# Results read back inside the merged scan and expert stage, and one PSUM bank for the up products with two for the down products

## The chip, the cores and the metric

The kernel runs on one core of a Trainium2 chip. The metric is the device time of one execution in microseconds; lower is better. Five engines run side by side, each working through its own queue in order: TensorE (PE; its weight loads are listed apart as PEld), VectorE (DVE), ScalarE (ACT), GpSimd (POOL), and SyncE (SP), which here only issues transfers. Work on one engine waits for work on another through semaphores. An engine whose next instruction waits does nothing else meanwhile.

## The reference

Eight layers over 4096 tokens of 128 numbers, each `x = layernorm(x + f(x))`. The change touches the last three:

```python
x = _layernorm(x + _L2_ffn_ref(x, ...))   # mixture of 8 experts, the best 2 of them per token
x = _layernorm(x + _L3_attn_ref(x, ...))  # selective state-space scan, see below
x = _layernorm(x + _L3_ffn_ref(x, ...))   # 8 dense experts, gated by top-p (0.8) probabilities

# _L3_attn_ref, shortened
x = resid * rsqrt(mean(resid**2) + EPS) * norm_w
skip = x @ skip_w.T;  xs = silu(causal_conv4(x @ in_w.T) + conv_b)
delta = softplus(xs @ wd1.T @ wd2.T + wd2_b)
h_l = exp(delta_l * A) * h_(l-1) + (delta_l * x_l) * B_l      # 16 states for each of 256 channels
y = (einsum(h, C) + xs * W_D) * silu(skip);  return resid + y @ out_w.T

# _L3_ffn_ref, shortened
h = relu(einsum('bth,ehf->betf', x, W1) + b1);  y = einsum('betf,efh->beth', h, W2) + b2
return einsum('bte,beth->bth', gate, y)
```

## The kernel before

The 4096 tokens are eight chunks of 512 (`NCH = 8`). `XT` holds the activations with the features on the partitions. PSUM has eight banks, `PS[0]` to `PS[7]`, each of 512 numbers per partition.

**Stage 6** is the expert mixture with two experts per token. It sorts tokens by expert into 72 tiles, and scatters each tile's result to DRAM (`result_d`) with indirect transfers from POOL. After the last tile comes a tail over the eight chunks: SP reads the two results of each token back (two transfers of 256 KB a chunk, into three buffers `YB`), DVE sums the two, PE turns the sum with four transposes, and DVE adds it to `XT` (`join`). A fence of all engines ends the stage.

**Stage 7** (`scan_moe_stage`) merges the last two layers. Everything in it is one list, `plan`, of steps; each engine walks the list and does its own part of each step, so the list fixes the order on every engine. After a prologue for chunks 0 and 1 it counts steps q from -8 to 319, and 32 steps make the scan of one chunk: for each of 16 states and 2 halves of the channels, ACT makes the decay (`decay`, an Exp of 128x512), POOL the input (`head`), DVE the scan (`scan`) and its product with C (`read`), POOL sums pairs (`pair`) and PE sums the rest in PSUM (`tail`, one product in each even step). The products of the dense experts begin at q = 60 (`first_unit`): 256 units (chunk i, expert x, quarter c), one a step. Unit u is `up` (three fp32r products of 512 columns), `hid` (ACT, a Relu out of PSUM), and `down` (one fp32 product, which is two instructions). Four units fill one `down` bank, and `gated` (DVE) and `join` (POOL) take it away.

In a step PE issues, in this order: `up(u+1)`, `tail`, the side steps, `down`. ACT issues `hid(u)`, the side steps, `decay`, and a `log` if there is one. `up` has two banks, `(PS[1], PS[4])`, and waits for the `hid` of two units before. `down` has one, `PS[2]`, so the first quarter of an expert is held back one step.

The side steps are everything else, put at fixed places by `put(q + n, ...)`: the preparation of the next chunk (`prepare`: conv, rank, delta, softplus, exp, log, dx), the skip gate (`skip_gate`), the end of a chunk (`hand_over`: output product, LayerNorm 7, routing), LayerNorm 6 two chunks ahead (`norm_ahead`), and LayerNorm 8 (`last_norm`). Nearly all of their products go to one bank, `PS[7]`. It is lent to the side steps in list order (`takers`); each waits in PE's queue until its predecessor's reader has let the bank go (`bank_free`). The readers are, for instance, `conv_out` for conv, `square`'s copy for centre, `softplus` (two Activates) for delta, `rows` for back, `row_out` for row, all of them on ACT.

Of the kernel before, what the change touches and what calls it, by code (L numbers as in the profile page):

```python
# [14 lines left out]
T = NB * L  # L15
# [147 lines left out]
def build(nc, wp, xT_d, sidx_d, cs_d, vecs_d, dc_d, pad_d, out_d):  # L163
# [36 lines left out]
    def w(name):  # L200
        r, o, c = at[name]
        return W[0:r, o:o + c]
# [1798 lines left out]
    def stage6():  # L2001
# [44 lines left out]
        zs, zt, zc = (Sig(sem("result_" + n), CK) for n in ("summed", "turned", "added"))  # L2046
        YB = [ax(1024) for _ in range(3)]
        h4 = lambda ap: ap.rearrange("p (h n k) -> p h n k", h=2, n=4)
        puts = lambda q: (s_put[q % YR], 32 * (q // YR + 1))
        arrived = lambda j: (s_rows_in[j % 8], 16 * (j // 8 + 1))  # L2050
        returned = lambda i: (s_back[i % 3], 32 * (i // 3 + 1))
        ph, pf, py = PS[1:4], PS[4:6], PS[6:8]

        def pe(e):
# [127 lines left out]
        def dve(e):  # L2182
# [52 lines left out]
            def join(i):  # L2235
                e.wait_ge(*zt.at(i))
                tt(ch(XT, i), PS[i % 4], ch(XT, i), ALU.add).then_inc(*zc(i))
# [23 lines left out]
        def sync(e):  # L2261
            regs = [nc.sync.alloc_register(f"tile_rows{j}") for j in range(8)]
            e.wait_ge(*tb.at("row"))
            e.wait_ge(*sent(6))
            e.wait_ge(*sent(7))
            for j in range(NTL):
                if j % 8 == 0:
                    nc.sync.reg_load(regs, trow[0:1, j:j + 8])
                    rows = [nc.sync.snap(r, min_val=0, max_val=XROWS - 128) for r in regs]
                if j >= 8:  # L2270
                    e.wait_ge(*gx.at(j // 4 - 2))
                    e.wait_ge(*gp.at(j // 4 - 2))
                nc.sync.dma_start(xg3[:, j % 8, :], sorted_d[bass.ds(rows[j % 8], 128), :]).then_inc(s_rows_in[j % 8], 16)
            weights(LATE).then_inc(s_w[LATE], 16)
            for q in range(NP - YR, NP):
                e.wait_ge(*puts(q))
            back = result_d[0:2 * T, :].rearrange("(h n p) d -> p h n d", h=2, p=128)
            for i in range(NCH):
                if i >= 3:
                    e.wait_ge(*zt.at(i - 3))  # L2280
                for h in range(2):
                    nc.sync.dma_start(h4(YB[i % 3])[:, h], back[:, h, 4 * i:4 * i + 4, :]).then_inc(s_back[i % 3], 16)
# [4 lines left out]
    def scan_moe_stage():  # L2287
# [11 lines left out]
        W1, W2 = w("W1"), w("W2")  # L2299

# [8 lines left out]
        hg = [ar(512) for _ in range(4)]  # L2309
# [3 lines left out]
        RW = ar(512, 8)  # L2313
# [4 lines left out]
        Ab, ups, po, Yp, misc = (PS[0], PS[3]), (PS[1], PS[4]), PS[2], PS[5:7], PS[7]  # L2318
# [3 lines left out]
        NORM = {6: ("centre", "square", "root", "norm", "back", "rows", "back2", "rows2"),  # L2322
# [62 lines left out]
        def norm_ahead(i, q):  # L2385
            n = norm(6, i)
            put(q + 17, n[0])
            put(q + 18, n[1])
            put(q + 20, n[2])
            put(q + 21, n[3])  # L2390
            put(q + 27, n[4])
            put(q + 28, n[5])
            put(q + 29, n[6])
            put(q + 30, n[7])
# [8 lines left out]

        both = lambda s: [(s, (0, 0)), (s, (0, 1))]
        plan = norm(6, 0) + both("conv")[:1] + both("conv2")[:1] + both("conv")[1:] + both("conv2")[1:] + both("conv_out")
        plan += both("shut") + norm(6, 1)[:3]
        plan += [("rank", 0), ("rank_out", 0)] + both("delta")
        plan += [("softplus", (0, 0)), ("softplus", (0, 1)), ("exp", 0), ("log", 0), ("dx", 0), ("rows_out", 0)]
        put(-2, norm(6, 1)[3])
        put(-1, *norm(6, 1)[4:])  # L2410
        for i in range(NCH + 1):
            q = 32 * i
            if i >= 1:
                hand_over(i - 1, q)
            if i < NCH:
                skip_gate(i, q)
            if i + 1 < NCH:
                prepare(i + 1, q)
            if i + 2 < NCH:
                norm_ahead(i + 2, q)  # L2420
            if i >= 2:
                last_norm(i - 2, q)
# [26 lines left out]
        for q in range(-8, first_unit + NU + 4):  # L2449
# [7 lines left out]
            plan += ahead(u + 1) + hidden(u)  # L2457
# [17 lines left out]
            plan += {0: [], 1: down(u - 2) + down(u - 1)}.get((u - 1) % 4, down(u - 1))  # L2475
# [9 lines left out]
        I = range(NCH)  # L2485
        rk_pe, rk_act, ex_act, ln_act, dl_dve, dx_pool, out_pe, res_dve = (
# [35 lines left out]
        for s, a in plan:  # L2522
            if s in ("open", "conv", "rank", "delta", "centre", "back", "back2", "logits", "out", "row"):
                takers.append((s, a))
        first_bank = {("conv", (0, 0)): 7, ("conv", (0, 1)): 5, ("rank", 0): 6, ("delta", (0, 0)): 7, ("delta", (0, 1)): 5,
# [6 lines left out]
        for t in takers:  # L2532
# [3 lines left out]
                  "out": res_dve, "row": rw_act}  # L2536
# [15 lines left out]
        def pe(e):  # L2552
            e.wait_ge(s_w[5], 16)
            for step, a in plan:
                if step == "centre":
                    n, i = a
                    bank_free(e, step, a)
                    if n == 7:
                        e.wait_ge(*res_dve.at(i))
                    elif n == 8:  # L2560
                        e.wait_ge(*join_pool.at((i, 7)))
                    for j in range(4):
                        r = mm(tile(bank(step, a), j), tile(XT, 4 * i + j), w("cen"))
# [16 lines left out]
                elif step == "back2":  # L2580
# [4 lines left out]
                    r.then_inc(*n_tr2(a))  # L2585
                elif step == "open":
# [76 lines left out]
        def scalar(e):  # L2663
# [3 lines left out]
            for step, a in plan:  # L2667
                if step == "square":
# [12 lines left out]
                    r.then_inc(*n_sq(a))  # L2681
                elif step == "norm" and a[0] < 8:
# [3 lines left out]
                    for j in range(4 if n == 6 else 0):  # L2686
                        act(tile(SB, j), tile(x, j), ACT.Copy, scale=root(i)[:, 4 + j:5 + j])
# [59 lines left out]
                elif step == "hid":  # L2747
# [5 lines left out]
                    act(hg[n % 4], ups[n % 2], ACT.Relu, bias=w("B1")[:, unit:unit + 1]).then_inc(*hid_act(a))  # L2753
# [71 lines left out]
        def dve(e):  # L2825
# [12 lines left out]
            for step, a in plan:  # L2838
                if step == "gate":
# [47 lines left out]
                elif step == "gated":  # L2887
# [6 lines left out]
                    stt(yg[q % 2], po, w("B2")[:, x:x + 1], gd[q % 3], ALU.add, ALU.mult).then_inc(*gy_dve(a))  # L2894
# [5 lines left out]
        def pool(e):  # L2900
            e.wait_ge(s_eps, 2)
            for step, a in plan:
# [13 lines left out]
                elif step == "dx":  # L2916
# [34 lines left out]
        def sync(e):  # L2951
            e.wait_ge(*dt_up.at(NTL - 1))
            nc.sync.dma_start(Wtap, vecs_d[2:3, :].partition_broadcast(128)).then_inc(s_conv, 16)
            for step, a in plan:
                if step == "rows_out":
# [211 lines left out]
```

## Time and profile before

| | |
|---|---|
| median of 3 runs | 2412.65 us (2411.06 to 2415.08) |
| profiled execution | 2396.13 us, of which 2394.3 us are the span from the first to the last instruction |
| PE / DVE / ACT / POOL busy over the span | 87% / 68% / 52% / 43% |
| mean granted TensorE clock | 0.925 of full speed |

Times below are microseconds from the span's start. Stage 6 ends near 1552 us, the steps of the scan run from about 1590 us, and the expert products from about 1738 us to the end. Full speed of the TensorE clock is 2.4 GHz; where the clock reads 0.5 it is 1.2 GHz. A line such as L209 is that of a helper that records every product, so groups are told apart by tile and shape. A matmul's start is stamped when it is handed on, up to one product early, so the distance between starts of groups is the better measure of its cost.

### The profile page before, as it was taken

How to read it: one execution, taken by the hardware profiler on the slowest of the kernel's cores; microseconds unless marked ns; L12 is line 12 of the kernel's file. 1: busy time of each engine (PE TensorE's matmuls, PEld its weight loads, DVE VectorE, ACT ScalarE, POOL GpSimd, SP SyncE). 2: the span in 40 equal slices, each digit the busy share in tenths (PEclk: the TensorE clock that was granted, in tenths of full speed). 3: DMA queues.
4: the chain of work that ended last, by engine and by line, in shares of the span. 5: the costliest groups of instructions: out<-in, count | busy, mean ns of one | idle time of the engine just before them, and what ended most of it. 6: DMA issues, size and time to landing. Idle time of an engine off the chain costs nothing.

```text
span 2394.3 us, 32522 instructions
## 1 busy us (share of the span) xinstructions
PE 2071.4 (87%) x11014; PEld 1515.0 (63%) x11014; DVE 1620.7 (68%) x3285; ACT 1235.2 (52%) x2694; POOL 1024.0 (43%) x911
## 2 busy tenths in 40 slices
PE   7888777899799999999999568556599998999998
PEld 3565656678689888888889557422254554555565
DVE  6657555677666667667676467548787888788921
ACT  6231222479644445445544334256567777766644
POOL 5000000121032232332333145358978889788922
PEclk9799899999999999999999689776699999999999
DMA  9500000000000000000000022523243343344311
GB/s 360 169 1 0 1 1 1 1 1 1 20 1 1 1 11 2 11 11 4 9 11 10 14 71 81 175 86 119 89 136 112 111 129 124 105 127 132 102 44 41
DMA packets 77148, 145.21 MB, mean 61 GB/s; under 512 B 9432, under 2 KB 31080, under 8 KB 75944
## 3 DMA queue, kind: packets, MB, share of 16 engines
q1 hardware_dynamic: 72600, 133.67, 17.6%
q0 software_dynamic: 4384, 9.46, 1.2%
q8 instruction: 89, 1.46, 0.3%
q14 instruction: 75, 0.61, 0.1%
HBM read 130.91 MB, written 31.65 MB: 68 GB/s over the span
## 4 chain that ended last, share of the span: by engine, by line
PE 60%; DVE 16%; POOL 9%; issue 6%; ACT 6%; DMA 1%; another core or an unknown queue 1%; SPq 0%; POOLq 0%; DVEq 0%; ACTq 0%
PE ps L209 55%; POOL TMP L233 6%; PE ps L216 5%; DVE ps L2863 2%; DVE TMP L229 2%; DVE TMP L232 2%; ACT TMP L224 1%; POOL XT L233 1%; DVE TMP L230 1%; DVE TMPr L229 1%; ACT TMP L225 1%; DVE SM L1183 1%; DVE XK L229 1%; DVE Wr L229 1%
## 5 line engine op out<-in xcount | busy, mean ns | idle before, releaser
L224 ACT ACTIVATE TMP<-ps,W 128x512 f32<-128x512 f32 (+2 forms) x784 | 456.6, 614 | 362.2 <-PE ps L209 180.3
L233 POOL TENSOR_TENSOR TMP<-TMP 128x512 f32<-128x512 f32 (+2 forms) x312 | 376.0, 1215 | 592.6 <-ACT TMP L224 443.6
L209 PE MATMUL ps<-TMP,W 128*128 128x512 f32 (+4 forms) x944 | 478.0, 622 | 61.9 <-POOL TMP L233 22.5
L209 PE MATMUL ps<-TMP 128*128 128x65 f32 (+5 forms) x4354 | 518.0, 287 | 6.9 <-DVE W L229 4.4
L209 PEld LDWEIGHTS ps<-TMP 128*128 128x128 f32 (+3 forms) x4354 | 477.5, 192 | 53.5 <-issue 16.6
L209 PEld LDWEIGHTS ps<-TMP,W 128*128 128x128 f32 (+2 forms) x944 | 179.4, 197 | 225.8 <-issue 126.2
L233 POOL TENSOR_TENSOR TMP<-TMP,W 128x512 f32<-128x512 f32 x256 | 313.8, 1248 | 9.1 <-DVE ps L2863 8.4
L209 PE MATMUL ps<-TMPr,Wr 128*128 128x512 f32 x768 | 302.6, 507 | 8.9 <-ACT TMP L224 8.7
L209 PE MATMUL ps<-TMPr 128*128 128x512 f32 (+4 forms) x1032 | 267.6, 405 | 34.0 <-DVE TMPr L229 23.1
L209 PEld LDWEIGHTS ps<-TMPr 128*128 128x128 f32 (+2 forms) x1032 | 193.5, 198 | 84.6 <-issue 23.2
L209 PEld LDWEIGHTS ps<-TMPr,Wr 128*128 128x128 f32 x768 | 144.2, 192 | 127.7 <-issue 88.6
L224 ACT ACTIVATE ps<-TMP,SM 128x512 f32<-128x512 f32 x256 | 176.6, 690 | 64.9 <-DVE TMP L229 59.9
L216 PE MATMUL ps<-W,TMP 128*128 128x128 f32 (+4 forms) x972 | 161.0, 284 | 56.1 <-DMA TMP<-sorted 22.4
L209 PE MATMUL ps<-Wr 128*128 128x512 f32 (+1 forms) x768 | 191.9, 366 | 18.1 <-DVE Wr L229 10.4
L227 ACT COPY TMP<-ps 128x260 f32<-128x260 f32 (+6 forms) x172 | 74.4, 436 | 226.3 <-PE ps L209 173.1
L2863 DVE TENSOR_TENSOR_SCAN ps<-ps,SM,TMP 128x512 f32<-128x512 f32 x128 | 164.4, 1285 | 9.7 <-ACT ps L224 9.6
L229 DVE TENSOR_TENSOR TMP<-W,ps 128x512 f32<-128x512 f32 x192 | 131.7, 686 | 54.8 <-PE ps L209 50.1
L2863 DVE TENSOR_TENSOR_SCAN ps<-ps,TMP 128x512 f32<-128x512 f32 x128 | 156.7, 1224 | 17.3 <-ACT ps L224 11.7
L216 PEld LDWEIGHTS ps<-W,TMP 128*128 128x128 f32 (+4 forms) x972 | 112.4, 144 | 88.3 <-issue 37.0
L229 DVE TENSOR_TENSOR TMPr<-ps,TMPr 128x512 fp32r<-128x512 f32 x118 | 81.3, 689 | 100.2 <-ACT TMPr L227 98.5
L209 PEld LDWEIGHTS ps<-Wr 128*128 128x128 f32 x768 | 119.3, 192 | 32.8 <-issue 15.4
L233 POOL TENSOR_TENSOR XT<-XT,TMP 128x512 f32<-128x512 f32 x72 | 91.8, 1275 | 107.2 <-DVE TMP L232 107.0
(241 smaller groups left out, 2939.2 us busy)
## 6 DMA issues: line engine op xcount, KB each, us to landing
W<-rows SPq DMA_DIRECT2D x224, 256.0 KB, 3.5
sorted<-pad SPq DMA_DIRECT2D x8, 2304.0 KB
XK<-gates SPq DMA_DIRECT2D x64, 256.0 KB, 3.6
TMP<-rows SPq DMA_DIRECT2D x32, 256.0 KB, 3.4
TMP<-sorted SPq DMA_DIRECT2D x72, 72.0 KB
W<-wp SPq DMA_DIRECT2D x1, 4124.0 KB
XK<-results SPq DMA_DIRECT2D x16, 256.0 KB, 3.7
W<-wp SPq DMA_DIRECT2D x1, 3072.0 KB, 25.5
```

The lines of the kernel that those rows point to most:

```text
L209: return nc.tensor.matmul(out, lhsT, rhs, start=start, stop=stop, **k)
L216: turn = lambda out, x, ident: nc.tensor.transpose(out, x, ident)
L224: return nc.scalar.activation(out, x, f, bias=bias, scale=scale)
L225: return nc.scalar.activation(out, x, f, bias=bias, scale=scale, accum_out=acc)
L227: acopy = lambda o, a: nc.scalar.copy(o, a)
L229: tt = lambda o, a, b, op: nc.vector.tensor_tensor(o, a, b, op)
L230: ts = lambda o, a, s1, s2, op0, op1=None: (nc.vector.tensor_scalar(o, a, s1, s2, op0, op1) if op1 is not None else nc.vector.tensor_scala ...
L232: stt = lambda o, a, s, b, op0, op1: nc.vector.scalar_tensor_tensor(out=o, in0=a, scalar=s, in1=b, op0=op0, op1=op1)
L233: gtt = lambda o, a, b, op: nc.gpsimd.tensor_tensor(o, a, b, op)
L1183: nc.vector.tensor_reduce(smax(u, 0), PSALL[0:112, 0:1024], AX, ALU.max).then_inc(*sc_max(u))
L2863: nc.vector.tensor_tensor_scan(Ab[x], Ab[x], Ub[q % 6], first, ALU.mult, ALU.add).then_inc(*h_dve(a))
```

## The change

- The tail of stage 6 is taken out. The read-back, sum, turn and add of chunks 0 and 1 stand in the prologue of stage 7 (`result_in`, `summed`, `turned`, `added`), those of chunks 2 to 7 two chunks ahead among the side steps, at q+7, q+10, q+12 and q+13 (`combine`). `turned` takes `PS[7]` there, between delta and back; its reader is DVE's add.
- `skip_gate` is put two steps later. POOL's product of `dx` becomes a step of its own, `dx2`, two steps after DVE's part and one behind `root`. ACT's first four copies of `norm` of LayerNorm 6 become `norm2`, and `norm` and the steps behind it keep their places or follow one later.
- `up` has one bank, `PS[1]`, and waits for the `hid` of the unit just before; `down` has two, `(PS[2], PS[4])`, and is issued every step. In a step PE now issues `tail`, the side steps, `down(u-1)`, and last `up(u+1)`.

```diff
-        zs, zt, zc = (Sig(sem("result_" + n), CK) for n in ("summed", "turned", "added"))
-        YB = [ax(1024) for _ in range(3)]
...
-            for i in range(NCH):
-                e.wait_ge(*zs.at(i))
-                if i >= 4:
-                    e.wait_ge(*zc.at(i - 4))
-                for j in range(4):
-                    r = turn(tile(PS[i % 4], j), tile(YB[i % 3], j), ident)
-                r.then_inc(*zt(i))
...
-            for i in range(NCH):
-                y = h4(YB[i % 3])
-                e.wait_ge(*returned(i))
-                tt(y[:, 0], y[:, 0], y[:, 1], ALU.add).then_inc(*zs(i))
-                if i > 0:
-                    join(i - 1)
-            join(NCH - 1)
...
-        Ab, ups, po, Yp, misc = (PS[0], PS[3]), (PS[1], PS[4]), PS[2], PS[5:7], PS[7]
+        Ab, up, pos, Yp, misc = (PS[0], PS[3]), PS[1], (PS[2], PS[4]), PS[5:7], PS[7]
...
-        NORM = {6: ("centre", "square", "root", "norm", "back", "rows", "back2", "rows2"),
+        NORM = {6: ("centre", "square", "root", "norm2", "norm", "back", "rows", "back2", "rows2"),
...
             put(q + 19, ("dx", i))
+            put(q + 21, ("dx2", i))
...
-            put(q + 18, ("open", (i, 0)))
-            put(q + 19, ("open_out", (i, 0)))
-            put(q + 20, ("gate", (i, 0)))
-            put(q + 21, ("open", (i, 1)))
-            put(q + 22, ("open_out", (i, 1)))
-            put(q + 23, ("gate", (i, 1)))
+            put(q + 20, ("open", (i, 0)))
+            put(q + 21, ("open_out", (i, 0)))
+            put(q + 22, ("gate", (i, 0)))
+            put(q + 23, ("open", (i, 1)))
+            put(q + 24, ("open_out", (i, 1)))
+            put(q + 25, ("gate", (i, 1)))
...
+        def combine(i, q):
+            put(q + 7, ("result_in", i))
+            put(q + 10, ("summed", i))
+            put(q + 12, ("turned", i))
+            put(q + 13, ("added", i))
...
-            plan += ahead(u + 1) + hidden(u)
+            plan += hidden(u)
...
-            plan += {0: [], 1: down(u - 2) + down(u - 1)}.get((u - 1) % 4, down(u - 1))
+            plan += down(u - 1) + ahead(u + 1)
...
-                    if n >= 2:
-                        e.wait_ge(*hid_act.at(units[n - 2]))
+                    if n >= 1:
+                        e.wait_ge(*hid_act.at(units[n - 1]))
...
-                    mm3(ups[n % 2], (W1h[:, o], W1l[:, o]), xparts[i % 2]).then_inc(*up_pe(a))
+                    mm3(up, (W1h[:, o], W1l[:, o]), xparts[i % 2]).then_inc(*up_pe(a))
...
-                    if c == 0 and i + x:
-                        e.wait_ge(*gy_dve.at(experts[8 * i + x - 1]))
-                    mm(po, tile(W2, 4 * x + c), hg[nth[a] % 4], c == 0, c == 3).then_inc(*dn_pe(a))
+                    if c == 0 and 8 * i + x >= 2:
+                        e.wait_ge(*gy_dve.at(experts[8 * i + x - 2]))
+                    mm(pos[x % 2], tile(W2, 4 * x + c), hg[nth[a] % 4], c == 0, c == 3).then_inc(*dn_pe(a))
```

## Rows read from the trace of the kernel before

**Rows 1.** Busy time by stretch: us, PE, PEld, DVE, ACT, POOL, clock, DMA.

```profile
1606.00:1738.00 132.00, 78.89 (x150) 29.96 (x149) 112.28 (x139) 76.07 (x165) 119.60 (x105) 0.70 0.33 106
1738.00:2277.00 539.00, 511.09 (x1609) 283.90 (x1610) 454.91 (x608) 379.16 (x789) 460.99 (x418) 0.98 0.39 120
2277.00:2387.00 110.00, 107.73 (x368) 65.42 (x368) 21.96 (x46) 50.46 (x97) 30.64 (x32) 1.00 0.13 40
...
1929.00:1978.00 49.00, 49.00 (x159) 27.37 (x158) 40.11 (x45) 34.72 (x83) 40.23 (x35) 1.00 0.47 133
1978.00:2021.00 43.00, 36.96 (x120) 20.10 (x120) 36.12 (x58) 33.27 (x75) 38.76 (x38) 1.00 0.34 107
```

**Rows 2.** What PE waited for from 1738 to 2262 us: total, times, longest.

```profile
PE ps L209 <- ACT XK L227: 10.5, 4, 2.7
PE ps L209 <- ACT TMP L224: 8.7, 7, 2.0
PE ps L209 <- DVE TMP L232: 6.6, 4, 3.5
```

**Rows 3.** Timeline of the second half of one chunk (start, us, engine, group, idle before).

```profile
1977.18 0.69 ACT L224 ACTIVATE TMP<-ps,W 128x512 f32<-128x512 f32 x1 [0.24 <-PE ps L209]
...
1987.18 1.12 PE L209 MATMUL ps<-XK,W 128*128 128x512 f32 x2 [2.72 <-ACT XK L227]
...
1988.29 2.37 POOL L233 TENSOR_TENSOR TMP<-TMP 128x1024 f32<-128x1024 f32 x1 [3.39 <-DVE TMP L229]
...
1989.14 0.67 ACT L224 ACTIVATE TMP<-ps,W 128x512 f32<-128x512 f32 x1
...
1996.55 2.45 ACT L224 ACTIVATE XK<-XK,SM 128x128 f32<-128x128 f32 x8 [3.50 <-POOL SM L233]
...
2000.42 0.95 PE L209 MATMUL ps<-TMPr,Wr 128*128 128x512 f32 x3 [1.32 <-ACT TMP L224]
...
2001.21 1.02 PE L209 MATMUL ps<-TMP,W 128*128 128x512 f32 x2
```

**Rows 4.** Timeline from the tail of stage 6 to the first centring of stage 7.

```profile
1530.21 14.96 SPq L2282 DMA_DIRECT2D XK<-results  x16
1533.83 0.69 DVE L229 TENSOR_TENSOR XK<-XK 128x512 f32<-128x512 f32 x1 [10.10 <-DMA XK<-results]
...
1534.58 1.12 PE L216 MATMUL ps<-W,XK 128*128 128x128 f32 x4 [11.89 <-DVE XK L229]
...
1552.54 2.08 PE L209 MATMUL ps<-W,XT 128*128 128x128 f32 x8 [0.83 <-DVEq L250]
```

**Rows 5.** Timeline of two waits in the steps ahead of the expert products.

```profile
1724.15 2.45 ACT L224 ACTIVATE XK<-XK,SM 128x128 f32<-128x128 f32 x8 [7.46 <-POOL SM L233]
1727.21 1.29 DVE L2863 TENSOR_TENSOR_SCAN ps<-ps,SM,TMP 128x512 f32<-128x512 f32 x1 [2.38 <-ACT ps L224]
```

**Rows 6.** Timeline of one step of the expert products after the scans.

```profile
2345.24 1.26 PE L209 MATMUL ps<-TMPr,Wr 128*128 128x512 f32 x3
...
2346.34 1.02 PE L209 MATMUL ps<-TMP,W 128*128 128x512 f32 x2
2346.54 0.69 ACT L224 ACTIVATE TMP<-ps,W 128x512 f32<-128x512 f32 x1 [0.87 <-PE ps L209]
...
2346.80 1.26 PE L209 MATMUL ps<-TMPr,Wr 128*128 128x512 f32 x3
```

**Rows 7.** Timeline of side steps in the first half of a chunk.

```profile
1936.82 1.27 ACT L224 ACTIVATE TMP<-ps,SM 128x512 f32<-128x512 f32 x2 [1.03 <-PE ps L209]
...
1938.17 1.96 PE L209 MATMUL ps<-XK,W 128*128 128x512 f32 x4
...
1959.85 0.59 ACT L227 COPY XK<-ps 128x512 f32<-128x512 f32 x1 [1.92 <-PE ps L209]
...
1971.71 0.60 PE L216 MATMUL ps<-W,XK 128*128 128x128 f32 x4
1972.07 0.94 PE L209 MATMUL ps<-TMPr,Wr 128*128 128x512 f32 x3
```

More of the change, by code:

```diff
@@ L2274, in sync @@
             weights(LATE).then_inc(s_w[LATE], 16)
[L2275 to L2282, printed above, removed]
         return dict(pe=pe, dve=dve, act=scalar, pool=pool, sync=sync)
@@ L2299, in scan_moe_stage @@
         W1, W2 = w("W1"), w("W2")
+        h4 = lambda ap: ap.rearrange("p (h n k) -> p h n k", h=2, n=4)
+        returned = lambda i: (s_back[1], 32) if i == 1 else (s_back[0], 32 * max(1, i))
         sets = [tuple(ar(1024) for _ in range(4)) for _ in range(2)]
@@ L2308, in scan_moe_stage @@
         xparts = [(ar(512, dt=FR), ar(512, dt=FR)) for _ in range(2)]
-        hg = [ar(512) for _ in range(4)]
+        HG, YB = ar(2048), ar(1024)
+        hg = [ch(HG, j) for j in range(4)]
+        rows_of = lambda i: HG[:, 0:1024] if i == 1 else YB
         yg = [ar(512) for _ in range(2)]
@@ L2390, in norm_ahead @@
             put(q + 21, n[3])
[L2391 to L2394, printed above, removed]
+            put(q + 22, n[4])
+            put(q + 27, n[5])
+            put(q + 28, n[6])
+            put(q + 29, n[7])
+            put(q + 30, n[8])
         def last_norm(i, q):
@@ L2402, in last_norm @@
             put(q + 42, n[4])
+        def combine(i, q):
[3 more added lines that the diff above has]
+            put(q + 13, ("added", i))
         both = lambda s: [(s, (0, 0)), (s, (0, 1))]
-        plan = norm(6, 0) + both("conv")[:1] + both("conv2")[:1] + both("conv")[1:] + both("conv2")[1:] + both("conv_out")
+        combined = lambda i: [("summed", i), ("turned", i), ("added", i)]
+        plan = [("result_in", 0), ("result_in", 1)] + combined(0) + norm(6, 0)[:3] + combined(1) + norm(6, 0)[3:] + both("conv")[:1] + both("conv2")[:1] + both("conv")[1:] + both("conv2")[1:] + both("conv_out")
         plan += both("shut") + norm(6, 1)[:3]
         plan += [("rank", 0), ("rank_out", 0)] + both("delta")
-        plan += [("softplus", (0, 0)), ("softplus", (0, 1)), ("exp", 0), ("log", 0), ("dx", 0), ("rows_out", 0)]
-        put(-2, norm(6, 1)[3])
-        put(-1, *norm(6, 1)[4:])
+        plan += [("softplus", (0, 0)), ("softplus", (0, 1)), ("exp", 0), ("log", 0), ("dx", 0), ("dx2", 0), ("rows_out", 0)]
+        put(-2, *norm(6, 1)[3:5])
+        put(-1, *norm(6, 1)[5:])
         for i in range(NCH + 1):
@@ L2485, in scan_moe_stage @@
         I = range(NCH)
+        zs, zt, zc = (Sig(sem("result_" + n), I) for n in ("summed", "turned", "added"))
         rk_pe, rk_act, ex_act, ln_act, dl_dve, dx_pool, out_pe, res_dve = (
@@ L2522, in scan_moe_stage @@
         for s, a in plan:
-            if s in ("open", "conv", "rank", "delta", "centre", "back", "back2", "logits", "out", "row"):
+            if s in ("open", "conv", "rank", "delta", "centre", "back", "back2", "logits", "out", "row", "turned"):
                 takers.append((s, a))
-        first_bank = {("conv", (0, 0)): 7, ("conv", (0, 1)): 5, ("rank", 0): 6, ("delta", (0, 0)): 7, ("delta", (0, 1)): 5,
+        first_bank = {("conv", (0, 0)): 7, ("conv", (0, 1)): 5, ("rank", 0): 6, ("turned", 0): 4, ("turned", 1): 4, ("delta", (0, 0)): 7, ("delta", (0, 1)): 5,
                       }
@@ L2535, in scan_moe_stage @@
         let_go = {"open": gt_dve, "conv": ev_act, "rank": rk_act, "delta": ab_act, "back": n_xa, "back2": n_xk,
-                  "out": res_dve, "row": rw_act}
+                  "out": res_dve, "row": rw_act, "turned": zc}
         bank = lambda s, a: PS[bank_no(s, a)]
@@ L2561, in pe @@
                         e.wait_ge(*join_pool.at((i, 7)))
+                    else:
+                        e.wait_ge(*zc.at(i))
                     for j in range(4):
@@ L2585, in pe @@
                     r.then_inc(*n_tr2(a))
+                elif step == "turned":
+                    bank_free(e, step, a)
+                    e.wait_ge(*zs.at(a))
+                    for j in range(4):
+                        r = turn(tile(bank(step, a), j), tile(rows_of(a), j), w("ident"))
+                    r.then_inc(*zt(a))
                 elif step == "open":
@@ L2681, in scalar @@
                     r.then_inc(*n_sq(a))
+                elif step == "norm2":
+                    i = a[1]
+                    x = scratch[6] if own_copy(a) else bank("centre", a)
+                    e.wait_ge(*n_rt.at(a))
+                    for j in range(4):
+                        act(tile(SB, j), tile(x, j), ACT.Copy, scale=root(i)[:, 4 + j:5 + j])
                 elif step == "norm" and a[0] < 8:
@@ L2685, in scalar @@
                     e.wait_ge(*n_rt.at(a))
-                    for j in range(4 if n == 6 else 0):
-                        act(tile(SB, j), tile(x, j), ACT.Copy, scale=root(i)[:, 4 + j:5 + j])
                     for j in range(4):
@@ L2838, in dve @@
             for step, a in plan:
-                if step == "gate":
+                if step == "summed":
+                    y = h4(rows_of(a))
+                    e.wait_ge(*returned(a))
+                    tt(y[:, 0], y[:, 0], y[:, 1], ALU.add).then_inc(*zs(a))
+                elif step == "added":
+                    e.wait_ge(*zt.at(a))
+                    tt(ch(XT, a), bank("turned", a), ch(XT, a), ALU.add).then_inc(*zc(a))
+                elif step == "gate":
                     i, x = a
@@ L2915, in pool @@
                     route_pool(e, step, a)
-                elif step == "dx":
+                elif step == "dx2":
                     sk, xs, dl, dx = sets[a % 2]
@@ L2953, in sync @@
             nc.sync.dma_start(Wtap, vecs_d[2:3, :].partition_broadcast(128)).then_inc(s_conv, 16)
+            for q in range(NTL // 2 - YR, NTL // 2):
+                e.wait_ge(s_put[q % YR], 32 * (q // YR + 1))
+            back = result_d[0:2 * T, :].rearrange("(h n p) d -> p h n d", h=2, p=128)
             for step, a in plan:
-                if step == "rows_out":
+                if step == "result_in":
+                    if a >= 2:
+                        e.wait_ge(*zt.at(a - 1 if a > 2 else 0))
+                    for h in range(2):
+                        nc.sync.dma_start(h4(rows_of(a))[:, h], back[:, h, 4 * a:4 * a + 4, :]).then_inc(s_back[int(a == 1)], 16)
+                elif step == "rows_out":
                     e.wait_ge(*rk_act.at(a))
```

12 lines of the change are left out of this document (4 added, 8 removed).

## The prediction

> **What bounds the kernel now.** I read first the busy shares by stretch. Before the expert products start, DVE and POOL are the full engines (112.3 and 119.6 of 132 us) and PE has room. From 1738 to 2277 us, where scans and expert products run together, PE is busy 511.1 of 539 us. In the last 110 us it is busy 107.7. Inside a chunk of the middle stretch the first half is PE without a gap (49.0 of 49.0), and the gaps lie in the second half (37.0 of 43) [rows 1]. So from 1738 us on, whatever makes PE wait counts in full, and the present waits, 539 - 511.1 = 27.9 us, are all that better side steps can give back.
>
> Second, the list of what PE waits for in that stretch: four waits of up to 2.7 us for a copy on ACT, others on `hid` and on DVE [rows 2]. Third, the timeline of a second half names them [rows 3]. The product of `open` waits 2.72 us for the copy of LayerNorm 6 that frees the side bank, since ACT is late. Then POOL waits 3.39 us for DVE's part of `dx`, and holds back `root`; ACT waits 3.50 us for it; and `up` waits 1.32 us for the `hid` behind.
>
> **The hand-over between the stages.** The read-backs start at 1530.21, the first sum runs at 1533.83 and the first transposes at 1534.58 for 1.12 us; the first centring of stage 7 comes at 1552.54 [rows 4]. After the change it waits only for the add of chunk 0, which follows its transposes: 1534.58 + 1.12 + 0.1 + 0.69 + 0.1 = 1536.6. That is 16.0 us sooner. The constants of stage 7 on DVE and ACT, which stood behind the fence, now fit in the wait before 1533.83. Chunk 1 is taken in while ACT squares chunk 0. Bounds: 14 to 17.
>
> **The six chunks in the loop.** Each costs SP two issues, DVE a sum and an add, and PE four transposes, 0.36 us from start to start [rows 7]. Four fall in the stretch that PE sets: 4 x 0.36 = +1.4. The other two fall where DVE is full, and cost 2 x 2 x 0.6 = +2.4. The transfers have three steps each before the sum, more than the 3.6 us from the first issue to the first sum [rows 4].
>
> **Open, dx2 and norm2.** In front of the expert products the same wait for `root` is 7.46 us long once, and 2.38 us of it reach the scan [rows 5]. There are two such passages, and I take some 3.7 us off each: -7.4, with the +2.4 above -5 for this stretch (-9 to +3). Behind 1738 us these edits can take away no more than the 27.9 us. I count all of those as gone and set the waits that I expect anew.
>
> **One bank for up, and up last in the step.** This is the costly part. A group of `up` takes 1.10 us to the next start and a `down` 0.46 more; together 1.56 us a step [rows 6]. Starts are stamped early, so I split it by the spacings when PE resumes: `up` 0.79 [rows 3], which holds 0.10 of weight load that is else hidden, so 0.69 in a stream; hence `down` is 0.86, and so is `tail`. `hid` starts 0.20 after `up` ends and lasts 0.69 [rows 6]. With some 0.05 for the signal the next `up` can start 0.94 after the last one ended. Four prices follow.
>
> (a) A step that holds only `down` and `up`: 0.94 + 0.79 = 1.73 in place of 1.56, +0.17. After the scans there are 54 such steps, 9.2, and about 1 more for squares and copies that come before a `hid` on ACT: +10 (5 to 14). In the middle stretch the odd steps without a side product, 29 of them: +4.9.
>
> (b) A side product whose bank is freed by ACT in the same step. Before, `up(u+1)` stood at the head of PE's step, so ACT did step u+1 while PE did step u, and the bank was free in time: the conv at 1938.17 starts as the two Activates of 1936.82 end [rows 7]. Now `hid(u)` starts after PE's step u-1, and the reader is behind it. PE reaches the product after nothing in an odd step and after 0.86 of `tail` in an even one. Two Activates (1.27) free the bank at 0.20 + 0.69 + 1.27 = 2.15, one copy (0.59) at 1.5. So each chunk's preparation pays: second conv 2.15 - 0.86 = 1.3, rank 1.5, second delta 0.6, logits 2.15; five chunks, 28. The new `turned`, lent the bank behind the first delta, pays 1.3 four times, 5. Back of LayerNorm 6 behind `row_out`: 1.5 four times, 6. The sum is 39, and 28 exposed weight loads of 0.10 make 2.8.
>
> (c) ACT over-full. From `hid` at 1977.18 to `hid` at 1989.14 ACT needs 12.0 us for three steps (split, exp, log, two table loads, square) [rows 3]. PE's work in these and the next is 2.41 + 2.40 + 2.41 + 1.55 = 8.8. With `up` tied to the `hid` just before, PE takes 0.2 + 12.0 + 0.74 + 0.79 = 13.7: 4.9 of waits, five times, the last without its square (-1.8): 22.7. `norm2` with `open_out`, then `norm`: about 1.2 four times, 4.8.
>
> Sum of the middle stretch: 4.9 + 39 + 2.8 + 22.7 + 4.8 = 74.2 new, +1.4 for the transposes, -27.9 old: +48. Lower bound +20, if ACT's queue hides half of (c) behind the waits of (b) and a third of (b) is covered; upper +65. The second bank of `down` removes a wait that is already avoided by holding a quarter back: 0.
>
> The Trainium skill (Perfetto Trace Analysis, Matmuls) says independent groups of matmuls should rotate through PSUM banks so that the evacuation of one overlaps the products of the next. It speaks against the single bank; with nothing in between, each of 256 units would lose 0.94 us, 240 in all. The trace does not bear out so much, since `down` covers 0.86 of it.
>
> **The sum.** -16 - 5 + 48 + 10 = +37 us. The profiled execution would go from 2396.1 to 2433; it lies 16.5 under the median of the runs, 2412.65, so the time to expect is 2412.65 + 37 = 2450.
>
> **The rivals.** *A, cover suffices (0.15):* the tails, side products and `down`, now ahead of `up`, hide the `hid`, and ACT keeps up. For it: 0.86 of 0.94 is covered even in the barest step. Then there remain -16, -5, the four waits of `open` (-10.5), some -4 for `root`, +1.4: -34, 2379 us. It decides at the logits step: if PE's wait there is under some 0.5 us in place of 2.15, this case holds. Against it: in a strict queue nothing of step u on ACT can start before `up(u)` is done.
>
> *B, the clock falls too (0.14):* where PE is busy 78.9 of 132 us the granted clock is 0.70, and it is 0.98 in the middle stretch [rows 1]. PE's share there would fall from 95% to about 87%. If a fifth of the middle stretch's waits bring 3 to 4 us each at 1.2 GHz, 10 to 30 us more: 2460 to 2480.
>
> *C, gains and losses cancel (0.05):* -16 - 5 + 20 + 5, within 5 us of before.
>
> The likeliest, +37 as summed, has 0.66, with 2425 to 2465 as its own range. The range over all is 2405 to 2485: A is left out but for its edge, and so is the far end of B. A measurement tells 0.2% (5 us) from nothing. Faster: A and a sliver of C, 0.16. Same: 0.05. Slower: 0.79.
>
> **What the profile after would show.** Right: the first centring of stage 7 some 16 us sooner; `open` with no wait; PE's idle time between the start of the expert products and the end of the scans at 60 to 80 us in place of 27.9, mostly on ACT; a bare step after the scans of 1.73 us in place of 1.56; gaps of 1.3 us ahead of `turned` and 2.1 ahead of the logits. Wrong: PE still busy over 94% there. The riskiest terms are (b) and (c), which assume that PE and ACT go in lockstep: were `hid` early, both would shrink together.

## The result, and the profile after

The kernel after takes 2461.15 us (median of 4 runs, 2460.32 to 2462.62), the kernel before 2411.86 us (4 runs, 2409.06 to 2415.08). The ratio is 1.0207, 95% interval 1.0193 to 1.0221: slower by 49 us. The forecast was 2450, range 2405 to 2485, with 0.79 for slower.

The two profiled executions differ by more, 2394.3 and 2460.8 us of span. 19.9 us of that lie ahead of the first read-back (1530.21 in [rows 4], 1550.07 now), that is ahead of anything the change moves; the last section says more on it. So I compare the rest by stretch, from landmarks that both programs have. "Row" is the first transpose of `row` of a chunk, the eight-column group that comes once in 32 steps. In us:

| stretch | before | after | difference | forecast |
|---|---|---|---|---|
| first read-back to first centring of stage 7 | 22.33 | 10.63 | -11.7 | -16 |
| first centring to row 0 (1734.24; 1743.72) | 181.70 | 183.02 | +1.3 | -5 |
| row 0 to row 6 (2270.01; 2324.47) | 535.77 | 580.75 | +45.0 | +48 |
| row 6 to the end | 124.3 | 136.3 | +12.0 | +10 |
| sum | 864.1 | 910.7 | +46.6 | +37 |

These are the profile after's busy times for the stretch before the expert products, with them, and behind the scans (us, then PE, PEld, DVE, ACT, POOL, granted clock, DMA share, GB/s):

```profile
1561.00:1744.00 183.00, 115.57 (x236) 47.95 (x236) 131.38 (x159) 103.31 (x231) 141.72 (x123) 0.70 0.33 102
1744.00:2324.00 580.00, 520.62 (x1606) 278.24 (x1605) 469.61 (x610) 371.12 (x781) 464.36 (x417) 0.98 0.37 115
2324.00:2454.00 130.00, 125.33 (x397) 65.78 (x395) 29.21 (x54) 55.96 (x107) 34.40 (x35) 1.00 0.14 37
```

From row 0 to row 6 PE is busy 521.4 us in place of 506.3, and so idle for 59.4 us in place of 29.5: 30 of the 45 us are idle time, and 15 are busy time. Part of that busy time is waiting too, since a step stretched by a short wait shows none before its `up` (the barest step below is 0.17 longer, and its product stands without an idle time). The clock there is the same 0.98. The list of what PE waited for from 1745 to 2325 us (total, times, longest) names who is late:

```profile
PE ps L209 <- ACT TMP L224: 31.5, 25, 2.9
PE ps L216 <- ACT TMP L227: 8.9, 5, 2.2
PE ps L209 <- ACT XK L227: 6.3, 5, 1.3
PE ps L209 <- DVE TMP L232: 5.4, 4, 3.1
PE ps L216 <- ACT TMP L224: 4.6, 4, 1.2
```

The list ends with five waits of 0.4 for ACT. It has 48 waits, 44 of them for ACT, where the same list of the kernel before has 17 (its longest entries are [rows 2]). The timeline of PE over one chunk shows them where they were forecast:

```profile
1991.81 2.81 PE L209 MATMUL ps<-TMP,W 128*96 128x512 f32 x6 [1.25 <-ACT XK L227]
2002.20 0.66 PE L216 MATMUL ps<-W,TMP 128*128 128x128 f32 x4 [1.20 <-ACT TMP L224]
2007.66 1.99 PE L209 MATMUL ps<-TMP,W 96*128 96x512 f32 x4 [0.40 <-ACT XT L227]
2012.27 1.06 PE L209 MATMUL ps<-W,XT 128*128 128x8 f32 x8 [1.94 <-ACT TMP L224]
...
2027.01 0.97 PE L209 MATMUL ps<-TMPr,Wr 128*128 128x512 f32 x3 [2.88 <-ACT TMP L224]
...
2047.81 0.66 PE L216 MATMUL ps<-W,XK 128*128 128x128 f32 x4 [1.62 <-ACT TMP L227]
2067.89 1.98 PE L209 MATMUL ps<-XK,W 128*128 128x512 f32 x4 [1.08 <-ACT TMP L224]
```

In this order: rank 1.25 (forecast 1.5), `turned` 1.20 (1.3), second delta 0.40 (0.6), logits 1.94 (2.15), `up` behind the over-full ACT 2.88, back 1.62 (1.5), second conv 1.08 (1.3). The reader is to see two sorts: a side product that waits for the bank, and `up` itself (`TMPr,Wr`). `open` still waits, against the forecast: its four waits of 0.4 to 3.1 us are the entry for DVE in the list.

The barest step, after the scans:

```profile
2403.02 0.96 PE L209 MATMUL ps<-TMPr,Wr 128*128 128x512 f32 x3
...
2403.81 1.02 PE L209 MATMUL ps<-TMP,W 128*128 128x512 f32 x2
2404.01 0.69 ACT L224 ACTIVATE TMP<-ps,W 128x512 f32<-128x512 f32 x1 [1.05 <-PE ps L209]
2404.75 0.53 PEld L209 LDWEIGHTS ps<-TMPr,Wr 128*128 128x128 f32 x3 [0.75 <-ACT TMP L224]
2404.75 0.96 PE L209 MATMUL ps<-TMPr,Wr 128*128 128x512 f32 x3
```

2404.75 - 2403.02 = 1.73 us, against 1.56 in [rows 6]. PE and ACT take turns: `hid` starts 0.20 after the start of the product behind `up`, lasts 0.69, and releases the next weight load 0.05 later.

### The profile page after: what moved, and what is told of

It reads as the page before. It is cut to its first block, busy times and chain, and to the rows that moved or that the text cites. A ratio compares the mean times of both kernels' runs of the same rounds, so it can differ in the third digit from the quotient of the medians.

```text
span 2460.8 us, 32524 instructions
## 1 busy us (share of the span) xinstructions
PE 2104.6 (86%) x11014; PEld 1516.0 (62%) x11014; DVE 1636.9 (67%) x3285; ACT 1231.7 (50%) x2694; POOL 1029.9 (42%) x911
## 3 DMA queue, kind: packets, MB, share of 16 engines
q1 hardware_dynamic: 72600, 133.67, 17.2%
## 4 chain that ended last, share of the span: by engine, by line
PE 62%; DVE 16%; ACT 8%; issue 6%; POOL 6%; another core or an unknown queue 1%; DMA 1%; POOLq 0%; SPq 0%; DVEq 0%; ACTq 0%
PE ps L209 57%; PE ps L216 5%; POOL TMP L233 4%; ACT TMP L224 3%; DVE TMP L229 2%; DVE ps L2866 2%; DVE TMP L232 2%; ACT L224 1%; DVE TMP L230 1%; DVE TMPr L229 1%; ACT TMP L225 1%; DVE SM L1183 1%; DVE Wr L229 1%; DVE XK L229 1%
## 5 line engine op out<-in xcount | busy, mean ns | idle before, releaser
L233 POOL TENSOR_TENSOR TMP<-TMP 128x512 f32<-128x512 f32 (+3 forms) x312 | 380.2, 1230 | 587.7 <-ACT TMP L224 457.0
L209 PE MATMUL ps<-TMP,W 128*128 128x512 f32 (+4 forms) x944 | 489.1, 622 | 56.8 <-POOL TMP L233 16.0
L209 PE MATMUL ps<-TMP 128*128 128x65 f32 (+5 forms) x4354 | 520.0, 288 | 6.8 <-DVE W L229 4.4
L209 PEld LDWEIGHTS ps<-TMP 128*128 128x128 f32 (+3 forms) x4354 | 479.4, 193 | 54.4 <-issue 17.9
L209 PE MATMUL ps<-TMPr,Wr 128*128 128x512 f32 x768 | 294.5, 492 | 18.2 <-ACT TMP L224 17.5
L209 PEld LDWEIGHTS ps<-TMP,W 128*128 128x128 f32 (+2 forms) x944 | 177.0, 197 | 197.9 <-issue 99.2
L209 PE MATMUL ps<-TMPr 128*128 128x512 f32 (+4 forms) x1032 | 267.3, 405 | 33.8 <-DVE TMPr L229 22.9
L209 PEld LDWEIGHTS ps<-TMPr,Wr 128*128 128x128 f32 x768 | 138.6, 191 | 183.5 <-ACT TMP L224 104.0
L209 PEld LDWEIGHTS ps<-TMPr 128*128 128x128 f32 (+2 forms) x1032 | 193.6, 198 | 83.9 <-issue 23.3
L216 PE MATMUL ps<-W,TMP 128*128 128x128 f32 (+4 forms) x1004 | 171.1, 290 | 86.3 <-DVE TMP L229 29.0
L209 PE MATMUL ps<-Wr 128*128 128x512 f32 (+1 forms) x768 | 195.4, 371 | 25.2 <-ACT TMP L224 14.9
L216 PEld LDWEIGHTS ps<-W,TMP 128*128 128x128 f32 (+4 forms) x1004 | 120.3, 149 | 125.0 <-issue 51.0
L229 DVE TENSOR_TENSOR TMP<-W,ps 128x512 f32<-128x512 f32 x192 | 131.6, 685 | 31.5 <-PE ps L209 26.1
L209 PEld LDWEIGHTS ps<-Wr 128*128 128x128 f32 x768 | 121.2, 195 | 40.2 <-ACT TMP L224 18.6
```

The costliest lines, as they stand in the source:

```text
L209: return nc.tensor.matmul(out, lhsT, rhs, start=start, stop=stop, **k)
L216: turn = lambda out, x, ident: nc.tensor.transpose(out, x, ident)
L229: tt = lambda o, a, b, op: nc.vector.tensor_tensor(o, a, b, op)
L233: gtt = lambda o, a, b, op: nc.gpsimd.tensor_tensor(o, a, b, op)
```

## The experiments

Ten kernels ran, one of them twice, in three groups, each group on its own chip and beside the kernel before. "Middle" is row 0 to row 6, "end" is row 6 to the last instruction; before has 535.8 and 124.3, after 580.8 and 136.3. Kernels of different groups are compared by these stretches, or by their ratios to the kernel before. The two stretches repeat well: one kernel, profiled on two chips, gave 534.5 and 534.8, 124.6 and 124.6. Medians do so less, so small differences are read from the stretches.

**1. After, with the old place and banks of `up`.**

```diff
-            plan += hidden(u)
+            plan += ahead(u + 1) + hidden(u)
...
-            plan += down(u - 1) + ahead(u + 1)
+            plan += {0: [], 1: down(u - 2) + down(u - 1)}.get((u - 1) % 4, down(u - 1))
...
-        Ab, up, pos, Yp, misc = (PS[0], PS[3]), PS[1], (PS[2], PS[4]), PS[5:7], PS[7]
+        Ab, ups, po, Yp, misc = (PS[0], PS[3]), (PS[1], PS[4]), PS[2], PS[5:7], PS[7]
```

(The two waits go back with it.)

> The changed kernel with the up and down products put back as before (two banks for up, one for down, up at the head of PE's step), all else as changed. Lockstep theory: the whole loss hangs on these edits, so the rest is a gain: -12 us for the hand-over, some -8 for open, dx2 and norm2: 2385 to 2400 us, no wait of PE over 1 us ahead of rank, turned or the logits. Rival (the added side steps in the full stretch cost by themselves): 2412 us or more.

Measured: 2384.36 us against 2400.68, ratio 0.9934 (0.9911 to 0.9957). Middle 534.5, end 124.6, the read-back to the first centring 10.64, from there to row 0 181.3. So the rest of the change is a gain, 16 us by the ratio and 13.1 from the first read-back to the end, and the whole loss hangs on `up` and `down`. Run again on another chip:

> The kernel with the old place and banks of `up`, timed again beside the two others. Ratio to the kernel before 0.991 to 0.996, as measured on it before; middle stretch 534 to 536 us.

Measured: 2356.71 against 2364.78, ratio 0.9973 (0.9955 to 0.9991), just above what was expected; that is 6 us. From the first read-back to the end it takes 853.3 us, the first time 851.0, before 864.1: 11 to 13 us less.

**2. Before, with the new place and banks of `up` and `down` alone** (the same lines the other way round).

> The kernel before with the change of the up and down products alone. Lockstep theory: +10 after the scans and +40 to +55 where scans and expert products run together, so 2460 to 2480 us, slower than the changed kernel itself or level with it. Rival (side steps cost): within 15 us of before.

Measured: 2459.42, ratio 1.0247 (1.0222 to 1.0271), +59 us; middle 578.2, end 136.3. That is the increase that was expected. That edit alone makes the loss.

**3. Place or banks.** Two kernels between after and the first one. One leaves `up` last in the step, with two banks (and `down` with one, a quarter held back):

```diff
-            plan += down(u - 1) + ahead(u + 1)
+            plan += {0: [], 1: down(u - 2) + down(u - 1)}.get((u - 1) % 4, down(u - 1)) + ahead(u + 1)
```

> The changed kernel with two banks for up and one for down again, but up still issued last in PE's step. Lockstep theory: the waits of side products for a reader on ACT in the same step (about 8 us a chunk) come from the place of up alone and stay, the bare step after the scans is back at 1.56 us: 2425 to 2440 us. Rival (the single bank is the whole cause): within 5 us of the first kernel of this group.

Measured: 2448.22, ratio 1.0203 (1.0178 to 1.0229); middle 591.6, end 127.5. That is more than the theory had it, and far from its rival. The other puts `up` first but leaves it one bank:

```diff
-            plan += hidden(u)
+            plan += ahead(u + 1) + hidden(u)
...
-            plan += down(u - 1) + ahead(u + 1)
+            plan += down(u - 1)
```

> The changed kernel with one bank for up and two for down, but up at the head of PE's step as before. Lockstep theory: the waits of side products in the first half of a chunk are gone, the bare step stays at 1.73 us (+10 after the scans), and ACT's full steps in the second half still hold up back (some 4 us a chunk): 2415 to 2435 us. Rival (the place of up is the whole cause): within 5 us of the first kernel of this group.

Measured: 2402.2, ratio 1.0005 (0.9988 to 1.0021); middle 540.5, end 133.4. That is less than the theory had it and more than its rival. What PE waited for from row 0 to row 6, first with `up` last and two banks, then with `up` first and one bank:

```profile
PE ps L209 <- DVE TMP L232: 31.8, 9, 5.4
PE ps L209 <- ACT TMP L224: 18.9, 14, 1.9
PE ps L216 <- ACT TMP L227: 7.7, 5, 2.2
PE ps L209 <- ACT XK L227: 6.3, 5, 1.3
PE ps L216 <- ACT TMP L224: 4.6, 4, 1.2
```

```profile
PE ps L209 <- ACT TMP L224: 27.6, 23, 2.3
PE ps L216 <- ACT TMP L227: 1.1, 1, 1.1
```

Against the first kernel the late place costs 2448.2 - 2384.4 = 64 us (60 in middle and end). Moving one bank from `up` to `down` costs 18 (15 in middle and end), and both together (ratio 1.0207 over 0.9934 or 0.9973) 56 to 66 (58). They don't add up: with `up` at the head the move of the bank costs 15 us of middle and end, with `up` last it costs nothing (10.8 us less in the middle, 8.8 more at the end). With `up` last, a second bank frees `up`, but the products of the side bank still wait in the same step (6.3 + 4.6 + 7.7, in the kernel after 6.3 + 4.6 + 8.9), because ACT can start nothing of step u before `up(u)`, which is PE's last work of the step before. The expectation was too low with `up` last, since a wait that I had not counted came on top: `down`, with its one bank, for `gated` on DVE:

```profile
2017.55 3.78 PE L209 MATMUL ps<-TMP,W 128*128 128x512 f32 x4 [4.78 <-DVE TMP L232]
```

There is one such wait of 4.5 to 5.4 us in each chunk, and the granted clock falls with it. Here are three stretches of 10 us around the one at 2220.70:

```profile
2206.00:2216.00 10.00, 9.29 (x27) 4.75 (x26) 8.21 (x11) 8.72 (x16) 10.00 (x9) 1.00 0.38 113
2216.00:2226.00 10.00, 5.30 (x8) 2.82 (x9) 9.76 (x25) 2.79 (x7) 9.81 (x12) 0.68 0.25 72
2226.00:2236.00 10.00, 10.00 (x33) 5.40 (x31) 8.00 (x10) 6.59 (x14) 6.95 (x6) 0.98 0.24 86
```

0.68 is 6.4 of 10 us at the lower level, 1.2 GHz. Over the middle stretch the clock is 0.96 here and 0.98 in the first kernel. 0.04 of 591.6 less 0.02 of 534.5 makes at most some 13 us of the 64 (an estimate from clocks of two digits; the engine was idle for part of the time at the lower level, so it is less). This is rival B, in a kernel with longer waits than the change has.

With `up` first, side products are free of waits but for one of 1.1 us, and what is left is `up` waiting for `hid`.

**4. The second bank of `down`.** `up` first with one bank, and `down` back to one bank with the quarter held back. Against the second kernel of (3) this takes the second bank from `down`; against the first kernel it takes the second bank from `up` and changes nothing else.

```diff
-            plan += down(u - 1)
+            plan += {0: [], 1: down(u - 2) + down(u - 1)}.get((u - 1) % 4, down(u - 1))
...
-                    if c == 0 and 8 * i + x >= 2:
-                        e.wait_ge(*gy_dve.at(experts[8 * i + x - 2]))
+                    if c == 0 and i + x:
+                        e.wait_ge(*gy_dve.at(experts[8 * i + x - 1]))
```

> One bank for up and one for down, up at the head of the step, all else as changed. It tells what the second bank of down gives. Theory (it ends PE's waits for DVE's gated, 20 us between 1725 and 2310 us in the kernel with one): 10 to 20 us more than with two down banks. Rival (holding a quarter back already avoids the wait, as predicted): within 3 us of it.

Measured: 2438.35 against 2414.38, ratio 1.0105 (1.0079 to 1.0130); middle 555.8, end 144.0. That is 15.3 and 10.6 us, and by the ratios 0.0100 x 2414 = 24 us, above the kernel with two banks of `down`, more than was expected. PE's lists for the middle (with two banks it was 27.6 in 23 waits) and for the end:

```profile
PE ps L209 <- ACT TMP L224: 36.9, 35, 3.2
```

```profile
PE ps L209 <- ACT TMP L224: 10.7, 14, 1.0
```

They are nearly all for `hid`, and none is for `gated`, so it is not the wait that the theory named. In a step without a `down`, `up` has less ahead of it that covers the `hid`, and the two in the next step don't give it back. The end bears this out: 12 of its 14 waits are 0.78 us long, there is about one for each expert, and together they are as long as the end has grown, 10.6 us (with two banks the end has 0.5 us of such waits). For the middle that reading is argued.

Against the first kernel the second bank of `up` is worth 21.3 us in the middle and 19.4 at the end, 41 in all. The 15 us of the second kernel of (3) are that price less the 26 us that the second bank of `down` gives back.

**5. The logits a step later.** After, with logits at q+16 in place of q+15, so that the bank's reader has a step of its own.

```diff
-            put(q + 15, n[6])
-            put(q + 16, ("logits_out", i), ("split", i))
+            put(q + 16, n[6], ("logits_out", i), ("split", i))
```

> The changed kernel with the logits product one step later (q+16), behind the step in which ACT frees the bank. Theory (a side product waits 1.9 us because its bank's reader on ACT stands behind the hid of the same step): that wait is gone in five chunks, and the stretch with scans and expert products is 5 to 10 us shorter than the changed kernel's 580.8; the other waits of side products stay as they are. Rival (PE only waits elsewhere instead): that stretch within 2 us of 580.8.

Measured: 2446.22 against 2414.38, ratio 1.0141 (1.0115 to 1.0166) in place of 1.0207; middle 566.8, so 13.9 us less, from five logits steps, where 5 to 10 were expected. The logits' waits of 1.94 are gone, and the list of waits for ACT by L209 falls from 31.5 to 22.3 us. The others stay as they were:

```profile
PE ps L209 <- ACT TMP L224: 22.3, 22, 2.9
PE ps L216 <- ACT TMP L227: 8.9, 5, 2.2
...
PE ps L209 <- ACT XK L227: 6.3, 5, 1.3
...
PE ps L216 <- ACT TMP L224: 4.5, 4, 1.2
```

So a same-step wait is a term by itself that one step of distance buys off. Idle time fell by 9.0 us (59.4 to 50.4); the other 4.9 are busy time, 516.6 in place of 521.4 us for the same 1609 products, at a clock of 0.99 for 0.98.

**6. Before, with the later open, `dx2` and `norm2` alone.**

> The kernel before with the later open, dx2 and norm2 alone. As predicted these gain 7 us ahead of the expert products and end the waits of open (10 us). The first group of runs speaks against so much: I now expect 3 to 8 us less than before in all, since PE waits for DVE's gated instead. Rival (they gain nothing): within 2 us of before.

Measured: 2409.4 against 2414.38, ratio 0.9996 (0.9979 to 1.0013): no difference is shown, and the 3 to 8 us that were expected are not. Middle 532.6, first centring to row 0 180.7: 3.2 and 1.0 us less. PE's waits for `open` are gone, and waits for DVE stand in their place, 20.3 us where [rows 2] has 6.6. The list from row 0 to row 6 sums to 30.5 us, before to 29.2:

```profile
PE ps L209 <- DVE TMP L232: 20.3, 8, 3.5
PE ps L209 <- ACT TMP L224: 9.3, 6, 2.1
PE ps L216 <- ACT TMP L227: 0.9, 1, 0.9
```

**7. The hand-over without POOL's drain.** The first kernel again; in the fence behind stage 6 POOL waits for the last scattered rows and writes one column, in place of a drain.

```diff
-            nc.gpsimd.drain().then_inc(s_fence, 1)
+            if landed:
+                for s, v in landed:
+                    e.wait_ge(s, v)
+                nc.gpsimd.memset(SM[:, 443:444], -0.5).then_inc(s_fence, 1)
...
```

> The kernel with the old up and down products and the new hand-over, and POOL's drain in the fence behind stage 6 replaced by waits for the landing of the last scattered rows. Theory (the drain after the indirect transfers sets when stage 7 begins, some 2.3 us behind the landing of the read-back and more with the constants that follow): the first centring comes 6.3 to 7 us after the first read-back in place of 10.6, so 4 us less than the first kernel of the first group, ratio to before about 0.992. Rival (the read-back's landing sets it): no difference.

Measured: the first centring comes 6.28 us after the read-back in place of 10.64, so 4.4 less. The whole, 2400.36 against 2414.38, ratio 0.9949 (0.9929 to 0.9969), lies between the two ratios of the kernel with the drain, so no gain in the total is shown. In the profiled execution the last write to DRAM hides it: the span ends 7.0 us after that write is issued (2392.05), and 2.6 to 2.8 us after it in every other kernel here. From the first read-back to the issue of that write it takes 845.5 us, with the drain 848.3 and 850.6. Why the write landed late in this one execution is not known. The two hand-overs, of the kernel after and of this one:

```profile
1550.07 2.04 SPq L2965 DMA_DIRECT2D TMP<-results  x4
1556.00 0.23 ACT L224 ACTIVATE SM<-W 128x32 f32<-128x32 f32 x1 [15.87 <-POOLq L258]
1556.00 0.17 DVE L231 TENSOR_SCALAR SM<-W 128x2 f32<-128x2 f32 x1 [10.66 <-POOLq L258]
...
1558.01 0.68 DVE L229 TENSOR_TENSOR TMP<-TMP 128x512 f32<-128x512 f32 x1
...
1558.83 1.09 PE L216 MATMUL ps<-W,TMP 128*128 128x128 f32 x4 [18.18 <-DVE TMP L229]
```

```profile
1546.57 2.04 SPq L2970 DMA_DIRECT2D TMP<-results  x4
1546.62 0.10 POOL L261 MEMSET SM<- 128x1 f32 x1 [1.40 <-DMA results<-TMP]
...
1550.14 0.69 DVE L229 TENSOR_TENSOR TMP<-TMP 128x512 f32<-128x512 f32 x1 [1.30 <-DMA TMP<-results]
```

With the drain, the other engines stand at the fence until 5.9 us after the read-backs are issued, and then DVE makes its constants (2.0 us) ahead of the first sum. Without it the constants are made while the rows arrive, and the sum waits for the transfer alone, 3.6 us after its issue.

**8. Can the waits for `gated` be bought off?** The first kernel still has 19.7 us of them. One kernel holds two quarters back, the other has DVE do `gated` a step sooner.

```diff
-            plan += {0: [], 1: down(u - 2) + down(u - 1)}.get((u - 1) % 4, down(u - 1))
+            plan += {0: [], 1: [], 2: down(u - 3) + down(u - 2) + down(u - 1)}.get((u - 1) % 4, down(u - 1))
```

> The kernel with the old place and banks of `up`, but the first quarters of an expert are held back two steps in place of one (three `down` together in the third). Theory (PE's remaining waits there are for `gated`, which DVE does late): they are 19.7 us in 7 waits of up to 3.5 us; a step more of 1.5 to 1.7 us leaves less than half. Middle stretch 534.5 -> 522 to 528 us, the whole some 8 us under the kernel with the old `up`, ratio to the kernel before 0.990. Rival (they are one lateness of DVE, and PE only meets it at another step or in `hid` waiting for `down`): within 3 us of it, 0.993.

```diff
-            plan += gated(u - 3) + joined(u - 4)
+            plan += gated(u - 2) + joined(u - 4)
```

> The same kernel with `down` as of old, but `gated` stands a step sooner in DVE's list. Theory: the same cover of one step given from the other side, middle stretch 522 to 530 us. Rival: DVE is behind by more than a step at these places, or now waits for PE itself in front of its scan; then nothing, 533 to 538 us.

Measured beside the repeat of the first kernel (2356.71): 2372.12 and 2374.39 us, ratios to before 1.0037 (1.0019 to 1.0055) and 1.0043 (1.0027 to 1.0058); middle 550.1 and 549.7 in place of 534.8. Both are misses for the theory, and worse than its rival had it. DVE's timeline in the first kernel shows what is late: once in a chunk the routing (a scan of 2.03 us, an operation of 1.15) stands in front of `gated` at 1985.55, and the `down` with the held quarter, four instructions, waits for it. That the routing is the cause is read from the timeline; no run moves it.

```profile
1981.08 2.03 DVE L2785 TENSOR_TENSOR_SCAN TMP<-TMP 128x32 f32<-128x32 f32 x1
1983.15 1.15 DVE L231 TENSOR_SCALAR TMP<-TMP 128x32 f32<-128x32 f32 x1
...
1984.41 1.23 DVE L2866 TENSOR_TENSOR_SCAN ps<-ps,TMP 128x512 f32<-128x512 f32 x1
1985.55 0.73 DVE L232 SCALAR_TENSOR_TENSOR TMP<-ps,W,XK 128x512 f32<-128x512 f32 x1
```

```profile
1986.33 3.62 PE L209 MATMUL ps<-TMP,W 128*128 128x512 f32 x4 [2.96 <-DVE TMP L232]
```

Held back two steps, PE meets the same lateness two steps on, at `open`, whose bank DVE's `gate` has to free:

```profile
1966.30 2.08 PE L209 MATMUL ps<-XK,W 128*128 128x512 f32 x2 [2.52 <-DVE TMP L232]
```

The total of the waits for DVE is unchanged (19.9 in 6 waits), and waits for ACT grow from 10.8 to 20.9 us. With `gated` sooner, the waits for `gated` do go (7.2 us are left, all at `open`), but those for ACT grow to 30.7, and four at a transpose for DVE are new (5.4). Why ACT comes later there was not followed further.

## Why the prediction was right, and where its terms were off

**The mechanism held.** `up` at the end of the step and tied to the `hid` just before puts PE and ACT in lockstep. The step of 1.73 us came to the hundredth; the six same-step waits came within 0.1 to 0.25 us of their prices; the idle time of the middle stretch, 59.4 us, lies just under the 60 to 80 named. The edit alone makes the loss (2), and without it there is a gain (1). The prediction did not separate place from bank; the runs do. The place alone costs the full amount, through (b), through `gated` and through a clock that falls with it. With `up` at the head, its second bank alone is worth 41 us in middle and end, of which the second bank of `down` gives 26 back.

The Trainium skill (Perfetto Trace Analysis, Matmuls) wants independent groups rotated through PSUM banks. The runs agree in direction, 41 us for taking the second bank from `up` and nothing else (4), far from the 240 us of nothing in between. But the kernel with `up` last has that rotation back and is still 64 us over the first. What bears on that is the statement of the Trainium skill ("PSUM — Partial Sum Buffer", Engine vs sequencer instructions) that matrix products start and complete in program order; these runs agree with it.

**The hand-over, -16: it was -11.7.** The step that failed is "waits only for the add of chunk 0". The fence was there before as well, but POOL's drain ended under the old tail. With the tail gone it is on the path, and so are 2.0 us of constants that I had placed inside the wait. Without the drain (7) the centring comes 6.28 us after the read-back, where the working had 1536.6 - 1530.2 = 6.4.

**Ahead of the expert products, -5: it was +1.3.** The first kernel and its repeat show -0.4 and +1.5, the later steps alone -1.0. So the 3.7 us that I took off each of two passages did not come; no row has the 3.7, and no run shows it. The added sums cost 0.6 to 2.5 us by these readings, where 2.4 was taken. Why the gain did not come is open: the two readings of one kernel differ by 1.9 us, which is too near to what is sought.

**The middle, +48: it was +45.0.** Its parts were off both ways, and that the sum came within 3 us is partly luck. (c) was too large: all waits of `up` in the middle are 17.2 us, where 22.7 and 4.8 were counted. The chunk shown has 2.88 + 0.76 + 0.35 = 4.0, where 4.9 and 1.2 were counted, probably because the waits of (b) leave ACT less behind when it comes there (not tried by itself). The old waits, -27.9, were counted as gone; but (6) and (1) show that moving `open` brings only 1 to 3 us, as DVE's lateness is met at `down` instead, and in the kernel after 5.4 us of waits for DVE are left at `open`. The term "second bank of `down`: 0" is the one that failed outright. With `up` at the head it is worth 26 us of stretches, between the kernels of (4) and (3). With `up` last PE waits 5.4 us for DVE in the kernel after, and 31.8 where `down` has one bank (and `up` two). These errors cancel in the sum. Of the 15 us that show as busy time, (a), the exposed weight loads and the transposes would be 4.9 + 2.8 + 1.4 = 9.1 by the forecast; the other 6 were not in the sum, and they were not followed.

**After the scans, +10: it was +12.0.** 54 steps of +0.17 are the 9.2 forecast; of the other 2.8, where 1 was counted, PE's list shows 2.4 in three waits for ACT, and the kernel before has none there.

**The rivals.** *A, cover suffices*, was to be decided at the logits step: 1.94 us, not under 0.5. *B, the clock falls too*, did not come: 0.98 before and after in the middle stretch, with PE's share at 90%. *C* is out by 45 us. What was missed above the forecast, 46.6 for 37, is the hand-over (4), the stretch ahead of the products (6) and the end (2), less 3 in the middle; the other 2.7 of the 49 us between the medians lie outside these stretches.

**The best version** is the change with `up` left as it was (1): 0.9934 and 0.9973 of the time before. Without the drain it measures the same within the intervals.

## What to carry to other kernels

Look for the product that another engine must read before it can do anything else in the step: it belongs at the head of PE's step, and its place can cost more than its second bank (60 us against 41 in middle and end). Where a product needs a bank that another engine lets go only late in the same step, it waits, and one step of distance removes the wait (13.9 us for five of them here). And when a wait or a tail is taken away, look for what ended under its cover: here a drain of POOL, and a routing step of DVE that PE then met somewhere else.

## What the runs showed of the hardware

POOL's drain behind indirect transfers: the last one is issued at 1547.75 and lasts 0.97 us; the read-backs, which wait for their data to be in DRAM, start at 1550.07; the drain ends only at 1556.00, 7.3 us after the last issue. The transfers themselves had been done for 6 us by then. The chain of waits of the kernel after has this as `1546.41 9.57 POOLq L258`.

One kernel, profiled on two chips, reached its first read-back at 1530.0 and at 1500.6 us, and the kernel before had medians of 2400.7, 2414.4 and 2364.8 us on three chips. From the read-back on the two profiles agree within 2.3 of some 852 us. Stages 1 to 6 are what varies; the granted clock from 900 to 1500 us was 0.95 and 0.94 in the two, so it does not explain the 29 us, and the cause stays open. The same holds for the 19.9 us ahead of the read-back between the two main profiles, whose chips are not on record: the total carries such differences, the stretches compared above do not.
